# Attention and gated feed-forward on one core: the scan and reciprocal of the next unit's running sums at the end of the vector engine's unit

## The reference, cut to what matters

```python
x = x + attn(layernorm(x))        # x: 4 sequences of 512 tokens, 512 features
x = x + ffn(layernorm(x))
# attn, 16 heads, for each sequence:
q, k, v, s, g = n @ Wq, n @ Wk, n @ Wv, clip(n @ Ws, -32, 32), n @ Wg
z  = cumlogsumexp(s, axis=time)   # running sums of exp(s)
# hk_t = hk * exp(z_{t-1} - z_t) + k_t p_t,  p = exp(s - z);   ok_t = q_t hk_t
# pv = softmax(ok);  hv_t likewise with v;                     ov_t = pv_t hv_t
o = rmsnorm_per_head(ov) * g_norm_weight * g * sigmoid(g)
return o @ Wo
# ffn: three products with weights rounded to fp8, silu(gate) * up
```

## Time and profile before

| what | before |
|---|---|
| time, median of 3 runs | 1505.59 us (1503.77 to 1508.01) |
| the profiled execution: its own time | 1505.37 us |
| its span | 1503.7 us |
| PE busy | 1431.0 us, 95% of the span |
| DVE busy | 1006.4 us, 67% |
| ACT busy | 433.3 us, 29% |
| POOL busy | 144.3 us, 10% |
| mean granted clock of PE | 0.992 of full speed |

### The profile page before, as it was taken

One profiled execution on the slowest core, in us unless ns is written; L12 is line 12 of the kernel. 1 busy time (PEld: TensorE's weight loads), 2 busy tenths in 40 slices (PEclk: granted clock), 3 DMA queues, 4 the chain that ended last, 5 costly groups with the idle time before them and its releaser, 6 DMA issues. The chain is left out here.

```text
span 1503.7 us, 23604 instructions
## 1 busy us (share of the span) xinstructions
PE 1431.0 (95%) x8480; PEld 1172.0 (78%) x8480; DVE 1006.4 (67%) x1619; ACT 433.3 (29%) x1243; POOL 144.3 (10%) x106
## 2 busy tenths in 40 slices
PE   7899999999999999999999999999999879999998
PEld 6777777777777787778777878787777758888886
DVE  8677776777677777776767776767677764535354
ACT  4323332333223323332323232323232222222221
POOL 3001110111011101110101110111010000000000
PEclk9999999999999999999999999999999989999999
DMA  5011002101110101020102100210000113000000
GB/s 168 20 58 39 22 23 62 39 18 37 42 39 18 50 29 39 18 60 25 32 18 60 31 26 18 61 32 25 18 17 1 57 57 146 29 0 28 0 29 28
DMA packets 61019, 57.23 MB, mean 38 GB/s; under 512 B 7297, under 2 KB 50049, under 8 KB 60929
## 3 DMA queue, kind: packets, MB, share of 16 engines
q1 hardware_dynamic: 60928, 55.87, 11.9%
HBM read 42.22 MB, written 13.63 MB: 37 GB/s over the span
## 5 line engine op out<-in xcount | busy, mean ns | idle before, releaser
L360 PE MATMUL bank<-wvg_hi,xT_hi 128*128 128x512 f32 x512 | 208.8, 408 | 0.0
L362 PE MATMUL bank<-wvg_hi,xT_lo 128*128 128x512 f32 x512 | 200.5, 392 | 0.0
L361 PE MATMUL bank<-wvg_lo,xT_hi 128*128 128x512 f32 x512 | 200.1, 391 | 0.0
L613 ACT ACTIVATE a_and_v<-bank 128x256 f32<-128x256 f32 x128 | 49.0, 383 | 294.4 <-PE bank L362 294.4
L964 DVE TENSOR_TENSOR y<-y,bank 128x512 f32<-128x512 f32 x128 | 87.7, 685 | 66.0 <-PE bank L362 65.8
L888 DVE SCALAR_TENSOR_TENSOR g<-tanh_half_g,bank 128x256 f32<-128x256 f32 x128 | 53.3, 417 | 94.2 <-ACT tanh_half_g L660 94.2
L832 POOL TENSOR_TENSOR rstd<-ssq,neg_half 128x8 f32<-128x8 f32 x32 | 52.4, 1636 | 656.3 <-DVE ssq L935 656.3
L360 PEld LDWEIGHTS bank<-wvg_hi,xT_hi 128*128 128x128 f32 x512 | 96.5, 188 | 21.3 <-issue 0.4
L362 PEld LDWEIGHTS bank<-wvg_hi,xT_lo 128*128 128x128 f32 x512 | 96.2, 188 | 20.8
L361 PEld LDWEIGHTS bank<-wvg_lo,xT_hi 128*128 128x128 f32 x512 | 96.6, 189 | 17.4
L360 PE MATMUL bank<-wo_hi,oT_hi 128*128 128x512 f32 x256 | 107.0, 418 | 1.5 <-DVE oT_lo L863 1.5
(11 more groups left out here) (157 smaller groups left out, 3215.5 us busy)
## 6 DMA issues: line engine op xcount, KB each, us to landing
fp_weights<-q SPq DMA_DIRECT2D x28, 318.0 KB, 2.6
stage_vg<-in_L_attn_Wv SPq DMA_DIRECT2D x32, 128.0 KB, 2.7
stage_vg<-in_L_attn_Wg SPq DMA_DIRECT2D x32, 128.0 KB, 3.2
stage<-in_L_attn_Wo SPq DMA_DIRECT2D x16, 256.0 KB, 2.7
out<-result SPq DMA_DIRECT2D x16, 256.0 KB, 2.1
y<-in_L_attn_hidden_states SPq DMA_DIRECT2D x3, 1024.0 KB, 9.0
w_down<-fp_weights SPq DMA_DIRECT2D x3, 1024.0 KB, 12.0
q<-in_L_ffn_gate_w SPq DMA_DIRECT2D x28, 106.0 KB, 2.0
```

The costliest lines, as they stand in the source:

```text
L360: pe.matmul(dst, w_hi, m_hi, start=(k == 0), stop=False)
L361: pe.matmul(dst, w_hi, m_lo, start=False, stop=False)
L362: last = pe.matmul(dst, w_lo, m_hi, start=False, stop=(k == n - 1))
L613: return act.activation(dst, src, ACT.Copy)
```

## The change

The call `sums(nu, ni)`, which stood between the two `times_gate` calls, is moved to the end of DVE's unit, behind `gate(2)` and `gate(3)`. Nothing is added or removed, and no other engine's order changes. The call happens at the end of units 0 to 30, so 31 of the 32 scans and reciprocals move; the one of unit 0 (in the head) stays.

```diff
                 if not tail:
                     quantise(u, slice(5, Q8_STEPS))
                 times_gate(u, i, 1)
-                if not last:
-                    sums(nu, ni)
                 times_gate(u, i, 0)
                 if tail:
                     norm_lo(i - 1, (0, 1))
                     norm_tokens(i - 1, (2, 3))
                 if not last:
                     gate(2, nu, ni)
                     gate(3, nu, ni)
+                    sums(nu, ni)
```

## The result

The changed kernel takes 1561.39 us (median of 4 runs, 1560.35 to 1562.02) against 1504.72 us for the kernel before in the same comparison. The ratio is 1.0372, 95% interval 1.0354 to 1.039: slower by 3.7%, 56.7 us. The forecast was 1556, with a range from 1534 to 1584.

What follows compares the result with a forecast made beforehand. PE, busy 95% of the span, was taken to bound the kernel, so its idle time counts. 1505.4 + 35.5 (later transposes, net of ST's gap) + 15 (clock drops) = 1556 us, range 1534 to 1584.

Steps and rivals of the forecast that it cites:

- The gain: PE's idle gap ahead of ST's first matmul (the s projection) goes in units 1 to 29: -35.2 us.
- the new wait: PE waits at the out transposes, ahead of KTJ: 2.34 us a unit, 67.9 us over the loop and unit 29.
- The chain: Scan and reciprocal delay `mean_square`, POOL, `out_norm` and PE's transposes: net +32.7 us through unit 29, +2.8 in units 30 and 31.
- The bounds from the tail, 1.90 and 0.84: Unit 31's times in us, applied to the loop: `mean_square` to `out_norm` through POOL, then `out_norm` to the first transpose.
- The sum: Whole kernel: 1505.4 + 35.5 for the delayed transposes + 15 for clock drops = 1556 us; chance 0.60.
- a clock that always falls: Rival: PE's clock falls behind nearly every wait at the transposes, +47 us, 1588 us in all; chance 0.10.
- The clock: PE's clock falls behind about 10 of 31 waits at the transposes, 1.5 us each: +15 us.
- faster: Rival: PE's gap at ST goes and the later `out_norm` stays hidden: 1470 us; chance 0.07.
- nothing measurable: Rival: saving at ST and wait at the transposes meet if `out_norm` is about 1.1 us earlier: 1505 us; chance 0.05.
- The chain-only case: Rival: PE waits at the transposes for the delayed `out_norm`, but the clock stays up: 1541 us; chance 0.18.

Runs made afterwards that it cites:

- experiment 2: Against the kernel before: scan moved to just ahead of `gate(2)`, reciprocal between `gate(2)` and `gate(3)`; 1459.99 us, ratio 0.9696.
- experiment 7: Changed kernel plus 8 filler matmuls ahead of the loop's out transposes and POOL's i=2 subtractions held until `out_norm` is done; 1542.68 us, ratio 1.0243.
- experiment 4: Changed kernel plus 8 unused filler matmuls on PE ahead of the out transposes in the loop's 28 units; 1549.39 us, ratio 1.0296.
- experiment 5: Changed kernel with POOL's three weight subtractions in units i=2 held until `out_norm` is done; 1556.79 us, ratio 1.0322.
- experiment 6: Changed kernel with the reciprocal over only 256 of the 512 columns, part of the computation left out; 1498.58 us, ratio 0.9939.
- experiment 3: Against the kernel before: scan and reciprocal moved together between `gate(2)` and `gate(3)`; 1472.48 us, ratio 0.978.
- experiment 1: Changed kernel with scan and reciprocal one instruction later, behind `mean_square` and ahead of the clip; 1506.53 us, ratio to the kernel before 1.0006.

## Why the prediction was right

**The gain** was as described: ST's gap goes, in every unit. Its size was a little low. I took the idle time that the profile prints, 1.01 us in the earlier trace rows. But ST's first matmul normally starts while the last transpose still runs: 1155.19 against 1154.84 + 0.60 = 1155.44, 0.25 us before its end. A gap costs its printed length and this overlap, 1.26 us. The starts of the transposes say the same: from one unit to the next they are 35.21 us apart in experiment 2 (682.37 to 717.58), where neither wait stands, and 36.46 in the kernel before (673.61 to 710.07) with its gap of 1.01. In the changed kernel they are 37.71 apart (780.32 to 818.03), so the new wait costs 2.50 us, where I had 2.34. I had both terms too small, and the errors nearly cancel.

**The chain** came out within 0.1 us at each link up to the transposes: 5.75, 7.61 and 8.44 us behind L448, where I had 5.75, 7.65 and 8.49. The bounds from the tail, 1.90 and 0.84, held for the loop.

**The sum** is settled by where the transposes of unit 29 start:

| kernel | start, us | difference |
|---|---|---|
| before | 1113.67 | |
| experiment 7 (chain alone) | 1142.64 | +29.0 |
| experiment 4 (and 7 collisions) | 1151.24 | +8.6, 1.2 each |
| changed (and 7 clock drops) | 1162.95 | +11.7, 1.7 each |

These are the transposes at the head of unit 29, in each profiled execution. The kernel before has one drop of its own in this stretch, at 1.5 us, so the chain is 30.5 and the clock 10.2 net. The term was 32.7 for the chain. Up to the end of the attention another 7.0 us come in: 2.7 from the chain in units 30 and 31 (I had 2.8), and about 4 from the clock, which falls three times there. Together that is 33.2 for the chain (I had 35.5), about 14 for the clock (15), and 8.6 for a third term that I did not have. That the forecast is within 6 us owes something to the first two being too large. The range was also wider than I said: its top holds 43 of the 47 us of a clock that always falls, and not two thirds of them.

**The clock** was forecast at 15 us from about 10 drops of 31. It was about 14 net, from 7 drops in the loop and 3 behind it, less the one of before. That the count fits is partly luck. It was one in three of the nearest rows, and which waits are followed by a drop hangs on more than their length: the profiled execution of experiment 5 has waits of the same 2.4 us with twice the drops, and experiment 6 has three drops with waits of 0.79 and 0.95 us. The rule that I took from the Trainium skill, "TensorE: Matmul & The Clock Gate", section "HAM oscillation — how this bites in real kernels", that a wait in every pass cuts the clock in every pass, isn't borne out here: 7 of 28 units of the loop in the changed kernel, and 15 in that execution. The page tells it of a loop whose waits for DMA are longer than the matmuls between them. This loop has a wait of 2.4 us in 37.7, so I had stretched the rule beyond its case.

**The step that was missing** is the collision with POOL, 8.6 us. I had moved `out_norm` to 7.65 us behind L448 and had not asked what POOL does at that time in units i=2. ACT's copy of the new weights follows the clip, through the exponential, and POOL's subtraction follows that copy. So the subtraction starts 1.95 us behind the clip in the kernel before (709.80 and 707.85), 1.93 in the changed one (739.27 and 737.34) and 1.95 in experiment 3. POOL before, in unit 18:

```profile
709.80 1.28 POOL L793 TENSOR_TENSOR ws_lo<-stage,ws_hi 128x512 fp32r<-128x512 f32 x1 [2.46 <-ACT ws_hi L613]
```

There `out_norm` followed the clip after 0.61 us and was done at 709.74, just ahead of the subtraction. In the changed kernel it waits for POOL's `rstd` and starts 1.83 us behind the clip, so the two meet. It is `out_norm` that has slid along, and not the clip: experiment 3 has the collision with an early clip, and experiment 1 has the late clip without it, since `out_norm` there follows the clip after 0.55 us. The Trainium skill, "SBUF — State Buffer", section "SBUF: two separate sides", states the rule behind it: a DVE instruction with two SBUF inputs and a GpSimd instruction that reads SBUF take turns on a shared port pair, the later one waiting for the whole of the earlier. The trace agrees: the second `out_norm` instruction, both of whose inputs lie in SBUF, takes 1.75 or 1.76 us in the 7 units instead of 0.68, and in unit 18 ends 0.56 us after POOL's. Experiment 1 shows the other order: POOL's `rstd`, 1.64 us in the changed kernel, starts 0.16 us behind the scan (700.44 to 701.66) and takes 2.49.

```profile
700.60 2.49 POOL L832 TENSOR_TENSOR rstd<-ssq,neg_half 128x8 f32<-128x8 f32 x1 [34.01 <-DVE ssq L935]
```

Of the rivals, "faster" was a matter of place. At `mean_square`'s side of the pair the two terms do meet (experiment 1, 1506.5), as the case "nothing measurable" said they would at 1.1 us: `out_norm` is 1.2 us earlier there. The chain-only case, 1541, is near experiment 7, 1542.7, though that has some 4 us of clock behind the loop in it.

## What to carry to other kernels

Work that nobody waits for belongs in a wait that the engine has anyway, and the wait must be chosen by what stands behind it in the queue. Here the same 4.5 us in each unit cost 57 us behind the last gate, nothing behind `mean_square`, and gained 46 us when split over the two waits for the tanh. An instruction that starts a round trip through another engine should be issued before any long work that doesn't feed it. When a step is moved in time, ask for every engine what it does at the new time, also for work that the change doesn't touch: here the step that slid was `out_norm`, and what it met was POOL's work for the next weights.

## What was unexpected of the hardware

- **Matmuls as filler made the kernel faster.** 224 matmuls of 512 columns in the waits took 12 us off (1561.4 to 1549.4), through the granted clock alone.
- **The clock falls behind some waits of 2.4 us and not behind others of the same length.** Experiment 5 shows both within 40 us. Its time scatters, 1552.9 to 1563.29 us over four runs, where experiment 7, whose profiled execution has no drop in the loop, has 1541.67 to 1545.06. But the changed kernel, with 7 drops, has 1560.35 to 1562.02. What tells the two kinds of wait apart was not settled by these runs.
- **DVE and POOL collide on 512-column fp32 work**, at 1.2 us of PE's time for each (experiment 4 less experiment 7). In unit 18 of the kernel before, `out_norm` had ended 0.06 us ahead of the subtraction.
